# Token norms: the inverse deviation as one power on GpSimd instead of a square root on ScalarE and a reciprocal on VectorE

## The chip, the core and the metric

The kernel runs on one NeuronCore of a Trainium2 chip. The core has five engines that run their own instruction streams and meet only at semaphores: TensorE (PE, matmuls), VectorE (DVE), ScalarE (ACT), GpSimd (POOL) and SyncE (SP, which mostly issues DMAs). The metric is the device time of one execution in microseconds, lower is better.

## The reference

Four layers of gated cross-attention and feed-forward act on a residual stream `x` of 128 x 64 = 8192 tokens of width 128. All eight sub-layers are different computations, but each of them reads a layer norm of the stream, and adds its result to the stream behind a gate:

```python
def _layernorm(x, axis=-1, eps=1e-05):
    m = jnp.mean(x, axis=axis, keepdims=True)
    v = jnp.var(x, axis=axis, keepdims=True)
    return (x - m) / jnp.sqrt(v + eps)

x = x + jnp.tanh(g_xattn[0]) * _L0_xattn_ref(_layernorm(x, axis=-1), ctx_1024, ctx_1024, ...)
x = x + jnp.tanh(g_ffn[0]) * _L0_ffn_ref(_layernorm(x, axis=-1), ...)
...
x = x + jnp.tanh(g_ffn[3]) * _L3_ffn_ref(_layernorm(x, axis=-1), ...)
```

What the change touches is `1 / sqrt(v + eps)`: one number for each token, eight times in the program. With 128 tokens to a tile and one token to a partition, the 8192 numbers are one tile of 128 partitions x 64 columns.

## The kernel before

The stream lives on chip as `X`, 128 partitions x 64 token tiles x 128 features. The program is a sequence of stages, one behind the other: `setup`, and then for each of the eight sub-layers a small stage `norm_header` and the stage or stages of the sub-layer itself. Each stage is a `Stage` object with its own buffers and semaphores, and inside it a block with one stream for each engine. At the end of the block all engines meet; then `Stage.__exit__` has the stage's semaphores cleared on GpSimd (L47) and all engines meet again (L48). No engine starts a piece of the next stage before that, its DMAs included. There is no scheduler: each engine's order is the order in which its function is written.

The sub-layer that last wrote `X` has also put each token's statistics (`bn_stats`: the means and the squared deviations of the even and the odd features) into `S6`. `norm_header` turns these into `m.mean` and `m.rstd`. On VectorE, seven small operations on 128 x 64 tiles (L179 to L187) leave the variance plus epsilon in `spread`. ScalarE waits for the third count of `step`, takes the square root of `spread` into `delta` (L194), and VectorE, which waits for `rooted`, takes the reciprocal of `delta` into `m.rstd` (L189). GpSimd, TensorE and SyncE have nothing to do in this stage. ScalarE's functions come in sets, and a set has to be loaded before its first use: the loads stand in the trace as ACT_TABLE_LOAD, placed by the compiler, with the line of the operation that they serve. The square root is in another set than what comes ahead of it and behind it.

The sub-layers read `m.mean` and `m.rstd` in `normed` (L200), the first piece of work on `X` in each of them.

The last sub-layer has layer norms of its own, in `gated_gelu`. There the inverse deviation of four tiles (128 x 4) is already taken as a power on GpSimd (L2487), with `half_power` a tile filled with -0.5 (L2481):

```python
pool.tensor_tensor(rstd[j][:], var[j][:], half_power[:], ALU.pow).then_inc(rooted[j], 1)
```

Of the kernel before, what the change touches and what calls it, by code (L numbers as in the profile page):

```python
# [12 lines left out]
ALU = mybir.AluOpType  # L13
ACT = mybir.ActivationFunctionType
AX = mybir.AxisListType.X

P = 128
S = 64
NB = 128
NT = NB * S // P  # L20
# [147 lines left out]
def norm_header(nc, m, name, s6=None):  # L168

    s6 = m.S6 if s6 is None else s6  # L170
    with Stage(nc, name) as st:
        delta, spread = st.sb("delta", [P, NT]), st.sb("spread", [P, NT])
        step, rooted = st.sem("step"), st.sem("rooted")

        mean_e, m2_e, mean_o, m2_o = (s6[:, :, k] for k in (1, 2, 4, 5))
        with nc.Block() as block:
            @block.vector
            def _(dve):
                dve.tensor_tensor(m.mean[:], mean_e, mean_o, ALU.add)  # L179
                dve.tensor_tensor(delta[:], mean_e, mean_o, ALU.subtract)  # L180
                dve.tensor_tensor(spread[:], m2_e, m2_o, ALU.add).then_inc(step, 1)
                dve.wait_ge(step, 1)
                dve.tensor_scalar(m.mean[:], m.mean[:], 0.5, None, ALU.mult)
                dve.scalar_tensor_tensor(delta[:], delta[:], 0.25, delta[:], ALU.mult, ALU.mult)
                dve.tensor_scalar(spread[:], spread[:], 1.0 / P, 1e-5, ALU.mult, ALU.add).then_inc(step, 1)
                dve.wait_ge(step, 2)
                dve.tensor_tensor(spread[:], spread[:], delta[:], ALU.add).then_inc(step, 1)  # L187
                dve.wait_ge(rooted, 1)
                dve.reciprocal(m.rstd[:], delta[:])  # L189

            @block.scalar
            def _(act):
                act.wait_ge(step, 3)
                act.activation(delta[:], spread[:], ACT.Sqrt).then_inc(rooted, 1)  # L194


def normed(dve, m, dst, t, src=None):
# [2412 lines left out]
def program(nc, d, stages=None):  # L2610
    with ExitStack() as ctx:
        m = Memory(nc, ctx)
        setup(nc, m, d)
        for n, stage in enumerate(STAGES):
            if stages is None or n in stages:
                norm_header(nc, m, f"norm{n}")
                with ExitStack() as own:
                    stage(nc, m, d, own)
        store(nc, m, d)
# [134 lines left out]
```

## Time and profile before

| what | value |
|---|---|
| median of 3 runs | 3924.22 us (3916.47 to 3931.73) |
| the profiled execution's own time | 3918.53 us |
| span of its instructions | 3916.6 us |
| TensorE busy | 3314.0 us, 85% |
| VectorE busy | 2456.6 us, 63% |
| ScalarE busy | 1686.4 us, 43% |
| GpSimd busy | 1167.3 us, 30% |

The span is what the trace covers, from the first instruction to the last; the execution's own time is 1.9 us longer. Busy shares are averages over very different stages: in a stage where all but one or two engines stand still, they tell nothing of what the stage waits for. The trace is read there in order of time.

### The profile page before, as it was taken

To read this page: it belongs to the slowest core of one execution; us is meant where nothing else is said; L and a number is where in the kernel's file an instruction comes from. 1 tells how busy PE (TensorE), PEld (TensorE's weight loads), DVE (VectorE), ACT (ScalarE), POOL (GpSimd) and SP (SyncE) were. 2 spreads that over 40 slices of the span, in tenths; PEclk is the share of its full clock that TensorE was granted. 3 is DMA by queue.
4 is the path that set the end of the run, shared out by engine and by line. 5 is a ranking of instruction groups with operands and counts; after the bars stand their busy time and mean duration, and the time that the engine had idled before them with its cause. 6 is when DMAs were issued, how large, how long until landed. Compare 5 with 4: busy or idle time off the path is not lost. (4 is left out here: it accounts for less than half of the span.)

```text
span 3916.6 us, 89814 instructions
## 1 busy us (share of the span) xinstructions
PE 3314.0 (85%) x31371; PEld 2123.4 (54%) x31371; DVE 2456.6 (63%) x5197; ACT 1686.4 (43%) x3144; POOL 1167.3 (30%) x1454
## 2 busy tenths in 40 slices
PE   3687999999688795589949997499999779999976
PEld 1464445444566542466646664266666446666644
DVE  7666111111688779878866676777776547777654
ACT  1333222222577536555512223266665226666522
POOL 1664000000233100044410003077775107777510
PEclk8766999999899897799959998799999899999988
DMA  4211000000000005011100002100000110000011
GB/s 131 59 40 51 0 0 0 0 0 0 17 13 13 4 16 226 16 54 45 32 17 1 0 0 74 53 10 9 9 9 4 35 32 10 9 9 9 4 35 56
DMA packets 163476, 107.80 MB, mean 28 GB/s; under 512 B 91390, under 2 KB 151980, under 8 KB 162348
## 3 DMA queue, kind: packets, MB, share of 16 engines
q1 hardware_dynamic: 161788, 104.02, 9.1%
q10 hardware_dynamic: 1584, 2.44, 0.2%
q8 instruction: 59, 0.97, 0.1%
q14 instruction: 45, 0.37, 0.0%
HBM read 68.52 MB, written 16.78 MB: 22 GB/s over the span
## 5 line engine op out<-in xcount | busy, mean ns | idle before, releaser
L2265 POOL TENSOR_TENSOR la_turned<-la_turned,la_sines 128x1024 f32<-128x1024 f32 x128 | 301.7, 2357 | 143.3 <-DVE la_sines L2191 143.3
L908 DVE TENSOR_TENSOR l0f_y<-A,l0f_s 128x512 f32<-128x512 f32 x16 | 11.1, 692 | 463.4 <-PE A L850 463.4
L2259 POOL TENSOR_TENSOR la_scaled<-la_turned,la_rlen 128x1024 f32<-128x1024 f32 x128 | 243.6, 1903 | 16.9 <-POOL la_rlen L2252 13.5
L1175 POOL COPY l1x_vd<-half 128x16 f32<-128x16 f32 x8 | 1.2, 212 | 605.8 <-POOLq L48 605.8
L2161 ACT ACTIVATE la_sq<-A 128x1024 f32<-128x1024 f32 x128 | 131.2, 1025 | 108.1 <-PE A L2311 81.6
L2183 DVE TENSOR_TENSOR la_turned<-A,la_cos 128x1024 f32<-128x1024 f32 x128 | 155.5, 1215 | 29.7 <-issue 15.4
L2145 ACT ACTIVATE la_prob<-la_prob 128x512 f32<-128x512 f32 x128 | 80.7, 630 | 204.1 <-DVE la_prob L2204 204.1
L2499 ACT ACTIVATE gg_gate<-B,gg_b 128x512 f32<-128x512 f32 (+1 forms) x96 | 65.9, 686 | 211.0 <-PE B L2525 211.0
L2201 DVE TENSOR_REDUCE la_top<-B 128x8 f32<-128x512 f32 x128 | 88.6, 692 | 108.4 <-PE B L2324 108.4
L2196 DVE TENSOR_REDUCE la_length<-la_sq 128x16 f32<-128x1024 f32 x128 | 155.1, 1212 | 0.0
L2331 PE MATMUL B<-la_wo,la_oT 128*128 128x128 f32 x1024 | 150.1, 290 | 2.7 <-ACT la_oT L2141 2.7
L2310 PE MATMUL A<-la_wq,la_hT 128*128 128x512 f32 x256 | 136.2, 615 | 11.2 <-DVE la_sines L2191 11.2
L2344 PE MATMUL A<-la_wv,la_hT 128*64 128x256 f32 x1024 | 139.6, 394 | 4.8 <-ACT la_qkT L2122 4.8
L2290 PE MATMUL A<-ident,la_scaled 128*128 128x128 f32 x1024 | 139.5, 279 | 4.4 <-issue 4.4
L2311 PE MATMUL A<-la_wk,la_hT 128*128 128x512 f32 x256 | 134.8, 609 | 0.0
L1506 POOL TENSOR_SCALAR l3x_factor<-l3x_raw 128x256 f32<-128x256 int32 x16 | 14.2, 890 | 398.8 <-DMA l3x_raw<-in_l3x_mask 397.6
L2331 PEld LDWEIGHTS B<-la_wo,la_oT 128*128 128x128 f32 x1024 | 125.5, 193 | 12.0 <-ACT la_oT L2141 3.6
L2524 PE MATMUL A<-gg_hT,gg_w 128*128 128x512 f32 (+1 forms) x192 | 106.1, 635 | 30.4 <-DVE l3f_y L2460 26.6
L2454 DVE SCALAR_TENSOR_TENSOR gg_hid<-A,gg_b,gg_gate 128x512 f32<-128x512 f32 (+1 forms) x96 | 72.0, 750 | 85.2 <-ACT gg_gate L2499 85.2
L2359 PEld LDWEIGHTS B<-la_vd,la_pT 64*64 64x64 f32 x4096 | 71.6, 134 | 97.3 <-issue 97.3
L2290 PEld LDWEIGHTS A<-ident,la_scaled 128*128 128x128 f32 x1024 | 110.0, 141 | 17.2 <-issue 10.4
L1184 POOL TENSOR_TENSOR l1x_kx<-l1x_kT,l1x_head_of 128x512 f32<-128x512 f32 x64 | 66.6, 1040 | 171.2 <-ACT l1x_kT L1303 171.2
(444 smaller groups left out, 9085.8 us busy)
## 6 DMA issues: line engine op xcount, KB each, us to landing
l1f_spill<-l1f_work SPq DMA_DIRECT2D x16, 768.0 KB, 3.2
l1f_xT<-l1f_spill SPq DMA_DIRECT2D x16, 768.0 KB, 6.1
l2x_ctx<-in_ctx SPq DMA_DIRECT2D x128, 64.0 KB, 2.2
memory_vd<-vd SPq DMA_DIRECT2D x64, 68.0 KB
X<-in_x SPq DMA_DIRECT2D x4, 1024.0 KB, 6.5
gates_rows<-in_ctx_rows SPq DMA_DIRECT2D x16, 256.0 KB, 2.8
memory_ctxT<-in_ctxT SPq DMA_DIRECT2D x64, 64.0 KB, 1.9
l1x_ctxT<-in_ctxT SPq DMA_DIRECT2D x64, 64.0 KB
```

The costliest lines, as they stand in the source:

```text
L2161: act.activation(sq[j % 2][:].rearrange("p n c -> p (n c)"), made[:], ACT.Square).then_inc(squared, 1)
L2183: dve.tensor_tensor(heads(turned[j % 2][:]), made_heads, cos[:, :, None, :].broadcast_to([P, 2, HEADS3, W3]), ALU.mult)\
L2196: dve.tensor_reduce(length[j % 2][:], sq[j % 2][:].rearrange("p n (h w) -> p (n h) w", h=HEADS3), AX, ALU.add).then_inc(summed, 1)
L2201: dve.tensor_reduce(top[j % 2][:], sim, AX, ALU.max).then_inc(max_done, 1)
L2259: pool.tensor_tensor(by_head(scaled), by_head(turned), spread_heads(rlen[j % 2][:], W3), ALU.mult)\
L2265: pool.tensor_tensor(turned[j % 2][:], turned[j % 2][:], sines[j % 2][:], ALU.add)\
L2290: last = pe.transpose(keyed[:, n * CH + g * P:n * CH + g * P + P], scaled[j % 2][:, n, g * P:g * P + P], m.ident[:])
L2310: pe.matmul(made[:, 0:CH], hT[j][:], wq[:], start=True, stop=True)
L2311: pe.matmul(made[:, CH:2 * CH], hT[j][:], wk[:], start=True, stop=True).then_inc(qk_made, 1)
L2331: last = pe.matmul(projected, oT[j % 2][:, g], wo[:, g], start=(g == 0), stop=(g == G - 1))
L2344: last = pe.matmul(made_v[u * S:u * S + S, b * G * W3:(b + 1) * G * W3], hT[j][:, b * S:b * S + S], wv[:].rearrange("p (g u w) -> p g u w" ...
L2524: pe.matmul(up_bank(j, o)[0:k], w1[:, n:n + k], hT[j][:], start=True, stop=True)
```

## The change

`norm_header` no longer uses ScalarE. A new tile `half_power` (128 x 64) is filled with -0.5 on GpSimd, which then waits for the third count of `step` and raises `spread` to the power -0.5, straight into `m.rstd`. VectorE's reciprocal and its wait on `rooted` are gone. The other seven operations of VectorE stand as before.

```diff
     with Stage(nc, name) as st:
         delta, spread = st.sb("delta", [P, NT]), st.sb("spread", [P, NT])
-        step, rooted = st.sem("step"), st.sem("rooted")
+        half_power = st.sb("half_power", [P, NT])
+        step, ready = st.sem("step"), st.sem("ready")
...
                 dve.wait_ge(step, 2)
                 dve.tensor_tensor(spread[:], spread[:], delta[:], ALU.add).then_inc(step, 1)
-                dve.wait_ge(rooted, 1)
-                dve.reciprocal(m.rstd[:], delta[:])
-
-            @block.scalar
-            def _(act):
-                act.wait_ge(step, 3)
-                act.activation(delta[:], spread[:], ACT.Sqrt).then_inc(rooted, 1)
+
+            @block.gpsimd
+            def _(pool):
+                pool.memset(half_power[:], -0.5).then_inc(ready, 1)
+                pool.wait_ge(ready, 1)
+                pool.wait_ge(step, 3)
+                pool.tensor_tensor(m.rstd[:], spread[:], half_power[:], ALU.pow)
```

Behind L189 the lines of the changed kernel have numbers that are one higher. Which instructions stand where in each engine's stream is shown at three places. The first is GpSimd around the second token norm, between the last operation of the first sub-layer (L524, L525 in the changed kernel) and the first branch of the next (L778, L779). ISA rows of L47 are the clearing of a stage's semaphores. Before:

```order
L521 TENSOR_TENSOR xnT<-xnT,memory_root 128x512
L524 TENSOR_TENSOR xnT<-xnT,norm_w 128x512
L484 UNCONDITIONAL_BRANCH
L47 ISA x2
L778 UNCONDITIONAL_BRANCH
L47 ISA
```

And in the changed kernel:

```order
L522 TENSOR_TENSOR xnT<-xnT,memory_root 128x512
L525 TENSOR_TENSOR xnT<-xnT,norm_w 128x512
L485 UNCONDITIONAL_BRANCH
L47 ISA
L190 UNCONDITIONAL_BRANCH
L192 MEMSET norm_half_power 128x64
L195 TENSOR_TENSOR rstd<-norm_spread,norm_half_power 128x64
L177 UNCONDITIONAL_BRANCH
L47 ISA
L779 UNCONDITIONAL_BRANCH
```

The fill and the power now stand between two clearings of semaphores, which before followed each other at once. The clearing that ends the norm's stage is behind the power on the same engine.

The second place is VectorE in the same stage. Before:

```order
L184 SCALAR_TENSOR_TENSOR norm_delta<-norm_delta 128x64
L185 TENSOR_SCALAR norm_spread<-norm_spread 128x64
L187 TENSOR_TENSOR norm_spread<-norm_spread,norm_delta 128x64
L189 RECIPROCAL rstd<-norm_delta 128x64
L176 UNCONDITIONAL_BRANCH
L722 UNCONDITIONAL_BRANCH
```

And in the changed kernel:

```order
L185 SCALAR_TENSOR_TENSOR norm_delta<-norm_delta 128x64
L186 TENSOR_SCALAR norm_spread<-norm_spread 128x64
L188 TENSOR_TENSOR norm_spread<-norm_spread,norm_delta 128x64
L177 UNCONDITIONAL_BRANCH
L723 UNCONDITIONAL_BRANCH
```

The reciprocal is gone, and VectorE goes from the addition to the end of the block.

The third place is ScalarE around the sixth token norm, between the attention of the third layer (its exponentials, L1316) and the router of its feed-forward part (L991, an exponential again). Before:

```order
L1289 COPY l2x_oT<-B 128x128 x2
L1150 UNCONDITIONAL_BRANCH
L191 UNCONDITIONAL_BRANCH
L194 ACT_TABLE_LOAD
L194 ACTIVATE norm_delta<-norm_spread 128x64
L176 UNCONDITIONAL_BRANCH
...
L988 UNCONDITIONAL_BRANCH
L991 ACT_TABLE_LOAD
L991 ACTIVATE route_inh<-l2f_mix 128x512
```

And in the changed kernel:

```order
L1290 COPY l2x_oT<-B 128x128 x2
L1151 UNCONDITIONAL_BRANCH
L763 UNCONDITIONAL_BRANCH
...
L989 UNCONDITIONAL_BRANCH
L992 ACTIVATE route_inh<-l2f_mix 128x512
```

Two loads are gone there: that of the square root, and that of the exponential behind it, whose set is still in place. At the seven other norms the square root's load is gone and the next sub-layer's own load stays. TensorE's and SyncE's streams are the same in both kernels.

## Rows read from the trace of the kernel before

**Rows 1.** The page's head: the span, and each engine's busy time.

```profile
span 3916.6 us, 89814 instructions
...
PE 3314.0 (85%) x31371; PEld 2123.4 (54%) x31371; DVE 2456.6 (63%) x5197; ACT 1686.4 (43%) x3144; POOL 1167.3 (30%) x1454
```

**Rows 2.** L187, L189, L194 by themselves: shortest, median, longest ns; first, last start.

```profile
L187 DVE TENSOR_TENSOR norm_spread<-norm_spread,norm_delta x8: 225/226/227, 27.7 to 2501.0; 128x64 f32<-128x64 f32 x8
...
L189 DVE RECIPROCAL rstd<-norm_delta x8: 552/553/554, 28.3 to 2501.5; 128x64 f32<-128x64 f32 x8
...
L194 ACT ACT_TABLE_LOAD  x8: 1283/1283/1283, 26.6 to 2499.8; - x8
L194 ACT ACTIVATE norm_delta<-norm_spread x8: 256/256/257, 28.0 to 2501.2; 128x64 f32<-128x64 f32 x8
```

**Rows 3.** Timeline, second token norm: start, us, engine, line, operation, idle before.

```profile
341.27 0.88 DVE L581 BATCH_NORM_STATS2 S<-X 128x6 f32<-128x128 f32 x4
343.03 1.28 ACT L194 ACT_TABLE_LOAD   x1 [5.99 <-PEq L48]
343.07 0.28 DVE L179 TENSOR_TENSOR mean<-S 128x64 f32<-128x64 f32 x1 [0.93 <-PEq L48]
...
344.20 0.23 DVE L187 TENSOR_TENSOR norm_spread<-norm_spread,norm_delta 128x64 f32<-128x64 f32 x1
344.46 0.26 ACT L194 ACTIVATE norm_delta<-norm_spread 128x64 f32<-128x64 f32 x1 [0.15 <-DVE norm_spread L187]
344.75 0.55 DVE L189 RECIPROCAL rstd<-norm_delta 128x64 f32<-128x64 f32 x1 [0.32 <-ACT norm_delta L194]
346.13 2.14 DVE L200 TENSOR_SCALAR l0f_turn_xn<-X,mean,rstd 128x128 f32<-128x128 f32 x8 [0.82 <-SPq L65]
...
347.30 2.15 PE L745 MATMUL A<-ident,l0f_turn_xn 128*128 128x128 f32 x8 [13.66 <-DVE l0f_turn_xn L200]
```

**Rows 4.** GpSimd's groups by line and shape: busy us, mean ns, idle before.

```profile
L504 POOL TENSOR_TENSOR memory_qx<-xnT,head 128x512 f32<-128x512 f32 x64 | 66.8, 1046 | 48.4 <-PE B L668 48.4
...
L2247 POOL TENSOR_TENSOR la_error<-la_error,la_length 128x16 f32<-128x16 f32 x128 | 28.4, 222 | 10.0
...
L277 POOL MEMSET vd<- 128x512 f32 x1 | 1.0, 1001 | 29.0 <-POOLq L48 29.0
L2481 POOL MEMSET gg_half_power<- 128x4 f32 x2 | 0.2, 101 | 36.8 <-POOLq L48 36.8
```

**Rows 5.** L2487 by itself: the powers that the kernel already takes.

```profile
L2487 POOL TENSOR_TENSOR gg_rstd<-gg_var,gg_half_power x32: 1006/1007/1037, 3046.9 to 3872.8; 128x4 f32<-128x4 f32 x32
```

**Rows 6.** Timeline around the first power.

```profile
3046.62 0.16 DVE L2439 TENSOR_TENSOR gg_var<-gg_var,gg_delta 128x4 f32<-128x4 f32 x1
3046.95 1.04 POOL L2487 TENSOR_TENSOR gg_rstd<-gg_var,gg_half_power 128x4 f32<-128x4 f32 x1 [10.93 <-DVE gg_var L2439]
3048.02 1.12 DVE L2445 TENSOR_SCALAR gg_h<-gg_hs,gg_mean,gg_rstd 128x128 f32<-128x128 f32 x4 [1.24 <-POOL gg_rstd L2487]
```

**Rows 7.** Windows behind five norms: us, busy by engine, granted clock, DMA, GB/s.

```profile
346.00:350.00 4.00, 2.45 (x10) 1.74 (x11) 3.53 (x14) 1.11 (x2) 0.00 (x0) 0.50 0.52 150
...
997.00:1000.00 3.00, 1.97 (x7) 1.48 (x7) 1.45 (x7) 0.00 (x0) 0.45 (x1) 0.50 0.31 86
...
1341.00:1345.00 4.00, 1.97 (x8) 1.58 (x9) 1.35 (x5) 1.88 (x3) 0.00 (x0) 0.50 0.01 2
...
1668.00:1673.00 5.00, 2.91 (x16) 1.67 (x24) 2.03 (x5) 0.53 (x2) 2.72 (x5) 0.50 0.39 104
...
2403.00:2408.00 5.00, 3.33 (x10) 2.29 (x11) 1.19 (x4) 1.17 (x2) 4.66 (x6) 0.50 1.01 208
```

**Rows 8.** Timeline at the start of the router's stage.

```profile
2007.89 1.28 ACT L991 ACT_TABLE_LOAD   x1 [3.60 <-PEq L48]
2007.93 0.16 DVE L952 RECIPROCAL l2f_temp<-l2f_temp 128x1 f32<-128x1 f32 x1 [0.81 <-PEq L48]
2008.13 0.49 DVE L953 TENSOR_SCALAR l2f_mix<-l2f_mix,l2f_temp 128x512 f32<-128x512 f32 x1
2009.19 0.63 ACT L991 ACTIVATE route_inh<-l2f_mix 128x512 f32<-128x512 f32 x1
```

**Rows 9.** Timeline of the first sub-layer: the same four transposes at two times.

```profile
35.50 1.12 PE L416 MATMUL A<-ident,gates_xn 128*128 128x128 f32 x4 [35.50 <-DVE gates_wk L350]
...
53.51 0.66 PE L416 MATMUL A<-ident,gates_xn 128*128 128x128 f32 x4
```

## The prediction

> **What bounds the kernel now.** The page's head says that TensorE is busy for 85% of the span [rows 1], but that average is of no use here. The change lies in eight short stages in which TensorE does nothing, so what counts is the timeline across one of them. Read [rows 3] downward. At 341.27 VectorE takes the last statistics of the first sub-layer; at 343.03 to 343.07 ScalarE and VectorE leave the barrier; VectorE works through its seven small operations until 344.20 + 0.23 = 344.43; ScalarE starts the square root at 344.46, VectorE the reciprocal at 344.75, which ends at 345.30; at 346.13 the next stage's first work on VectorE begins, and at 347.30 TensorE has its first matmul, after 13.66 us of idleness. Nothing else runs between 343.03 and 345.30, and no DMA of the next stage can be issued before the barrier. The norm's stage is therefore one chain of dependent steps, and each microsecond more or less in it moves everything behind it. Eight stages repeat the pattern with the same durations to a few ns [rows 2].
>
> The reader should also see what is not on that chain. ScalarE's table load takes 1283 ns [rows 2], but it starts at the barrier, side by side with VectorE, and ends at 344.31, 0.12 us before VectorE hands over its result [rows 3].
>
> **What is removed.** From the end of L187 to the end of the reciprocal: 345.30 - 344.43 = 0.87 us in each stage (a hand-over of 0.03, the square root 0.26, another 0.03, the reciprocal 0.55) [rows 2, 3]. The load of the square root's set is worth nothing, since VectorE's seven operations cover it; without that cover it would be worth its 1.28 us each time. One more load is gone, that of the router's exponential. There VectorE has the input ready at 2008.13 + 0.49 = 2008.62, the load ends at 2009.17, and the exponential starts at 2009.19 [rows 8]. With the set in place it could start 0.03 us behind VectorE, at 2008.65, so this saves 0.54 us, once.
>
> One rule speaks for a larger gain. The Trainium skill, ScalarE: Activation LUTs, section "What ACT_TABLE_LOAD costs", puts a switch to another set at about 2.66 us, of which some 1.38 us are a drain around the load. The trace agrees with the 1283 ns for the load, and shows no drain on the path: the square root starts 0.03 us after its input is there and 0.15 us after the load [rows 3]. By the page nine switches would be an estimated 24 us off the sum; by the rows they are 0.54 us. I take the rows.
>
> **What is added.** First the fill of `half_power`, 128 x 64, on GpSimd. Bounds from its neighbours are 101 ns for 128 x 4 and 1001 ns for 128 x 512 [rows 4]; on the line between them 64 columns are 0.21 us. It starts at the barrier and VectorE's seven operations last 344.43 - 343.07 = 1.36 us [rows 3], so it is hidden, at either bound; without this cover it would cost its 0.21 us.
>
> Second the hand-over from VectorE to GpSimd. In the existing use of the same pattern VectorE ends at 3046.78 and the power starts at 3046.95: 0.17 us [rows 6]. The barrier takes the place of the hand-over back.
>
> Third the power on 128 x 64, which is the whole question. The trace has it on 128 x 4 alone: 1007 ns, 32 times, from 1006 to 1037 [rows 5]. An ordinary two-input operation of GpSimd takes 222 ns on 128 x 16 and 1046 ns on 128 x 512 [rows 4], that is (1046 - 222) / 496 = 1.66 ns a column and 222 - 16 x 1.66 = 195 ns that do not depend on the size. So a power is no ordinary operation: on a quarter of the columns it takes 4.5 times as long as the 222 ns. How its 1007 ns split into a fixed part and a part for each column can't be read from one size, and 64 columns are 16 times as many as 4. The bounds:
>
> - All of the excess per column: (1007 - 195) / 4 = 203 ns a column, 0.195 + 64 x 0.203 = 13.2 us. If the fixed part is as small as the 101 ns of a tiny fill [rows 4], it is 227 ns a column and 14.6 us.
> - All of the excess fixed, and a column as cheap as in an ordinary operation: 1.007 + 60 x 0.00166 = 1.11 us.
>
> I take 13.2 us. The row that is nearest in kind, the ordinary operation, says that GpSimd's fixed part is some 0.2 us, and a logarithm, a product and an exponential are arithmetic that has to be done for each element. A set-up of 0.8 us, paid once whatever the size, would have no counterpart in any other row of this engine.
>
> **The sum.** Each stage gets longer by 0.17 + 13.2 - 0.87 = 12.5 us, eight of them by 99.8 us (with unrounded terms), less 0.54 us for the router: +99 us. Against the profiled execution's own 3918.5 us that is 4018 us. That execution stood 5.7 us below the median of the runs shown, 3924.2 us, so as a median I expect 4023 us, +2.5%. No cover exists for the 12.5 us: the clearing of the stage's semaphores is queued behind the power on GpSimd, the other four engines wait in the barrier for it, and `normed` (L200), the weights' DMAs and then TensorE are late by as much.
>
> **TensorE's clock** could add to this, since TensorE now idles some 26 us around the second norm in place of 13.66. But behind the norms it restarts at a granted clock of 0.50 (1.2 GHz) as it is: five such windows are in [rows 7], and the sixth and the eighth norm look the same. In the first sub-layer the four transposes take 1.12 us at 35.50 and 0.66 us at 53.51 [rows 9]; so the start is at the lower speed there too. A longer idleness takes nothing from a clock that is already down. When it comes back depends on chance as well, and I allow 10 us either way.
>
> **The rivals.**
> - **Part of the excess is fixed.** Say 0.4 us of the 0.81: then a column costs 103 ns, the power 7.2 us, a stage +6.5 us, the kernel +51 us: 3975 us. For it: some set-up (constants, a call) is likely for such a function. Against it: nothing in the trace shows one. I count powers from 3.2 to 10 us as this case.
> - **The power is nearly flat in size**, so the kernel is not slower. Its place is L195, its price 1.11 us, the lower bound above: 0.17 + 1.11 - 0.87 = +0.41 us a stage, +3.3 - 0.5 = +3 us in all, 3927 us. It decides from a power of 3.2 us downward (37 ns a column), where the eight stages give less than 20 us. For it: other two-input operations do have a slope of only 1.66 ns a column. Against it: it needs a fixed 0.66 us or more that no other GpSimd row has. The Trainium skill, GPSIMD Engine Reference, section 3.1, gives about 2.6 cycles an element for two-input operations, which would put the power here as well; the ordinary operations agree roughly with that, the power on 128 x 4 does not.
> - **The table loads were the real wait**, and the power is nearly flat besides: 9 x 1.28 us come back, 3927 - 11 = 3916 us or less; by the ScalarE page's figure some 24 us, 3903 us. For it: nine loads are gone. Against it: ends and starts in [rows 3] show them covered. For the kernel to be faster by more than 0.5%, both of these would have to hold.
> - **A first power has code to load.** GPSIMD Engine Reference, section 2.1, in the Trainium skill tells of some 6 us for a freshly loaded library. The first of the 32 powers took 1037 ns against a median of 1007 [rows 5], so the trace shows 0.03 us, and I leave it out.
>
> **How the numbers follow.** 0.5% of this time, 20 us, is about what a measurement of this kernel can tell from no change. The steep power (10 to 14.6 us, +74 to +111 us) has 0.60, the partly fixed one 0.22, the flat one 0.15, the loads 0.03. The first two are slower by over 0.5%: 0.82; same 0.15; faster 0.03. The forecast is the first case's, 4023 us. For 8 times in 10 the range has to hold the first two cases: its upper end is 3924 + 111 + 10 = 4045 us. Its lower end is 3950 us, where a power takes about 4 us; below that hardly any of the second case is left. The likeliest case by itself spans 3988 to 4045 us.
>
> **What the next profile would show.** L195: eight powers, each near 13.2 us (the sum is right), near 7 (partly fixed) or near 1.1 (flat). The eight durations should be equal to some tens of ns. The power should start 0.17 us behind VectorE's last addition, with all other engines idle under it. GpSimd's busy time grows by 8 x 13.4 = 107 us. ACT_TABLE_LOAD rows: nine fewer, without a gain beyond the router's 0.54 us. The idle time of TensorE ahead of its first matmul at the second norm grows from 13.66 to about 26 us. The prediction would be wrong if the power has a small slope, if something of the next stage starts under it, or if TensorE's clock comes back much earlier or later behind several norms.

## The result, and the profile after

The changed kernel takes 3992.99 us (median of 4, 3991.79 to 3999.28), the kernel before beside it 3920.34 us (median of 4). The ratio is 1.0185, with a 95% interval of 1.0158 to 1.0212: +73 us, slower. The forecast was 4023 us, +99 us. One execution of all those reported below, 4073.87 us in the kernel with the logarithm (mean granted clock 0.87, where the others of that kernel have 0.92), is in none of the ratios.

The page of the profiled execution after, head and busy times (as in [rows 1]):

```profile
span 3992.0 us, 89815 instructions
...
PE 3309.3 (83%) x31371; PEld 2120.1 (53%) x31371; DVE 2453.5 (61%) x5189; ACT 1672.0 (42%) x3127; POOL 1251.4 (31%) x1470
```

The span is 75.4 us longer, and the only engine with more work is GpSimd, by 84.1 us. The groups of its powers and of the fill by line and shape (busy us, mean ns, idle before), and below them the new power by itself (L2488 is the power that the kernel before has at L2487):

```profile
L195 POOL TENSOR_TENSOR rstd<-norm_spread,norm_half_power 128x64 f32<-128x64 f32 x8 | 84.5, 10564 | 11.2 <-DVE norm_spread L188 11.2
L2488 POOL TENSOR_TENSOR gg_rstd<-gg_var,gg_half_power 128x4 f32<-128x4 f32 x32 | 32.2, 1007 | 270.8 <-DVE gg_var L2440 270.8
L192 POOL MEMSET norm_half_power<- 128x64 f32 x8 | 1.2, 151 | 1442.4 <-POOLq L48 1056.7 <-ACTq L177 385.7
```

```profile
L195 POOL TENSOR_TENSOR rstd<-norm_spread,norm_half_power x8: 10549/10560/10583, 27.8 to 2567.2; 128x64 f32<-128x64 f32 x8
```

The power on 128 x 64 takes 10.56 us; the eight norms, with different data, lie within 0.04 us of each other. The timeline of the second norm, to be read beside [rows 3]:

```profile
352.62 0.15 POOL L192 MEMSET norm_half_power<- 128x64 f32 x1 [2.57 <-POOLq L48]
352.67 0.27 DVE L180 TENSOR_TENSOR mean<-S 128x64 f32<-128x64 f32 x1 [0.98 <-PEq L48]
...
353.80 0.23 DVE L188 TENSOR_TENSOR norm_spread<-norm_spread,norm_delta 128x64 f32<-128x64 f32 x1
354.18 10.58 POOL L195 TENSOR_TENSOR rstd<-norm_spread,norm_half_power 128x64 f32<-128x64 f32 x1 [1.40 <-DVE norm_spread L188]
365.61 2.14 DVE L201 TENSOR_SCALAR l0f_turn_xn<-X,mean,rstd 128x128 f32<-128x128 f32 x8 [11.59 <-SPq L65]
...
366.78 1.50 PE L746 MATMUL A<-ident,l0f_turn_xn 128*128 128x128 f32 x5 [23.60 <-DVE l0f_turn_xn L201]
```

From the first operation of the norm to the first `normed` it is now 365.61 - 352.67 = 12.94 us, where it was 346.13 - 343.07 = 3.06 us: +9.88 us in one stage. TensorE's wait ahead of its first matmul went from 13.66 to 23.60 us. Under the power all other engines stand still, so eight such stages are 79 us.

The traces bear that out for the whole program. Take in each norm the time from its first operation on VectorE (L179, L180 in the changed kernel) to the first operation on `X` that reads the inverse deviation. The eight such stretches, called the norms' stages from here on, add up to 49.9 us in the trace before and to 129.0 us in the trace after: +79.1 us. All the rest of the program takes 3866.8 us before and 3863.0 us after. The loss lies in the norms' stages and nowhere else.

The router, as in [rows 8]:

```profile
2062.96 0.48 DVE L954 TENSOR_SCALAR l2f_mix<-l2f_mix,l2f_temp 128x512 f32<-128x512 f32 x1
2063.48 0.63 ACT L992 ACTIVATE route_inh<-l2f_mix 128x512 f32<-128x512 f32 x1 [4.35 <-DVE l2f_mix L954]
```

No load stands ahead of the exponential any more, and it starts 0.04 us behind its input, where it had started 0.57 us behind it: 0.53 us back, once.

### The profile page after: what moved, and what is told of

It is laid out like the page before. It is cut to its first block and busy times, and to the rows that moved or that the text cites. A ratio compares the mean times of both kernels' runs of the same rounds, so it can differ in the third digit from the quotient of the medians.

```text
span 3992.0 us, 89815 instructions
## 1 busy us (share of the span) xinstructions
PE 3309.3 (83%) x31371; PEld 2120.1 (53%) x31371; DVE 2453.5 (61%) x5189; ACT 1672.0 (42%) x3127; POOL 1251.4 (31%) x1470
## 5 line engine op out<-in xcount | busy, mean ns | idle before, releaser
L2488 POOL TENSOR_TENSOR gg_rstd<-gg_var,gg_half_power 128x4 f32<-128x4 f32 x32 | 32.2, 1007 | 270.8 <-DVE gg_var L2440 270.8
```

## The experiments

The theory (A): the whole loss is the power's own duration on a path that nothing covers, a fixed part and a part for each column. Its rivals were another law of the size (B), a price of the move to GpSimd as such (C), table loads that had been on the path after all (D), and a price of TensorE's longer idleness in its clock (E).

### The law of the size

```diff
-                pool.tensor_tensor(m.rstd[:], spread[:], half_power[:], ALU.pow)
+                w = {"norm0": 1, "norm1": 2, "norm2": 4, "norm3": 8, "norm4": 16, "norm5": 32, "norm6": 48}.get(name, 64)
+                for n in range(0, NT, w):
+                    cols = slice(n, min(n + w, NT))
+                    pool.tensor_tensor(m.rstd[:, cols], spread[:, cols], half_power[:, cols], ALU.pow)
```

> The eight token norms of the changed kernel take the same 64 columns of powers in pieces, one behind the other: 64 pieces of 1 column in the first norm, 32 of 2 in the second, 16 of 4, 8 of 8, 4 of 16, 2 of 32, 48 + 16 in the seventh, and 64 in one in the eighth. The result is the same. Theory A (a fixed 0.37 us and 159 ns a column, the straight line through 1.007 us at 4 columns and 10.56 us at 64): 0.53 us for 1 column, 0.69 for 2, 1.01 for 4, 1.64 for 8, 2.92 for 16, 5.46 for 32, 8.0 for 48. Rival B (a column costs 203 ns when there are few and less when there are many, with 0.2 us fixed, a curve): 0.40 for 1, 0.60 for 2, and above the line in between, 1.8 for 8, 3.4 for 16.

GpSimd's groups of this kernel, by shape:

```profile
L198 POOL TENSOR_TENSOR rstd<-norm_spread,norm_half_power 128x1 f32<-128x1 f32 x64 | 32.4, 540 | 1.4 <-DVE norm_spread L188 1.4
L198 POOL TENSOR_TENSOR rstd<-norm_spread,norm_half_power 128x2 f32<-128x2 f32 x32 | 21.1, 697 | 1.4 <-DVE norm_spread L188 1.4
...
L198 POOL TENSOR_TENSOR rstd<-norm_spread,norm_half_power 128x4 f32<-128x4 f32 x16 | 15.7, 1008 | 1.4 <-DVE norm_spread L188 1.4
L198 POOL TENSOR_TENSOR rstd<-norm_spread,norm_half_power 128x16 f32<-128x16 f32 x5 | 14.4, 2899 | 1.4 <-DVE norm_spread L188 1.4
L198 POOL TENSOR_TENSOR rstd<-norm_spread,norm_half_power 128x8 f32<-128x8 f32 x8 | 12.8, 1637 | 1.4 <-DVE norm_spread L188 1.4
L198 POOL TENSOR_TENSOR rstd<-norm_spread,norm_half_power 128x32 f32<-128x32 f32 x2 | 10.8, 5431 | 1.4 <-DVE norm_spread L188 1.4
L198 POOL TENSOR_TENSOR rstd<-norm_spread,norm_half_power 128x64 f32<-128x64 f32 x1 | 10.6, 10574 | 1.4 <-DVE norm_spread L188 1.4
L198 POOL TENSOR_TENSOR rstd<-norm_spread,norm_half_power 128x48 f32<-128x48 f32 x1 | 8.0, 8019 | 1.4 <-DVE norm_spread L188 1.4
```

The eight sizes lie on one straight line, each within 0.04 us of theory A's number. From 4 to 64 columns the slope is (10574 - 1008) / 60 = 159 ns a column, and 1008 - 4 x 159 = 0.37 us don't depend on the size; the step from 1 to 2 columns is 157 ns as well. B is out. The kernel as a whole took 4042 us in its one run: the 0.37 us are paid 129 times in place of 8, which by this line is 45 us.

### The move without the power

```diff
-                pool.tensor_tensor(m.rstd[:], spread[:], half_power[:], ALU.pow)
+                pool.tensor_tensor(m.rstd[:], spread[:], half_power[:], ALU.mult)
```

> The changed kernel with the power replaced by a multiplication by half_power, so the inverse deviation is not computed (the norms are scaled wrongly). All else is as in the changed kernel: hand-over to GpSimd, the fill, nine table loads fewer, no reciprocal. Theory A (all of the loss is the power's own duration): a 128x64 multiplication takes 0.3 us, each stage gets 0.17 + 0.30 - 0.87 = -0.40 us, the kernel -3.7 us against before, the same within noise. Rival C (moving work to GpSimd and its barrier costs something of its own): slower than before. Rival D (the table loads had been on the path): 11 us or more faster than before.

3909.65 us (median of 10) against 3919.26 us (13), ratio 0.9974 [0.9964, 0.9985], that is -10.2 us [-14.1, -5.9]. The multiplication by itself:

```profile
L195 POOL TENSOR_TENSOR rstd<-norm_spread,norm_half_power x8: 317/318/319, 27.7 to 2490.6; 128x64 f32<-128x64 f32 x8
```

With 0.32 us on GpSimd the kernel is faster than before, so the move as such costs nothing and C is out. The gain is larger than the 3.7 us that A gives it, which is why the table loads were tried by themselves below. In the norms' stages the price is A's: they add up to 46.8 us in this trace, 3.1 us less than in the first trace of before (A: 8 x 0.40 = 3.2). The rest of the gain lies outside the norms.

### Half the columns, and the power twice

```diff
-                pool.tensor_tensor(m.rstd[:], spread[:], half_power[:], ALU.pow)
+                pool.tensor_tensor(m.rstd[:, 0:32], spread[:, 0:32], half_power[:, 0:32], ALU.pow)
```

(and on VectorE, behind the last addition, `dve.tensor_copy(m.rstd[:, 32:64], spread[:, 32:64])`)

> The changed kernel with the power on 32 of the 64 columns; the other half of the inverse deviations is a copy of the variance made by VectorE beside it, so half of the tokens are scaled wrongly. Theory A (duration on the path, a line in the size): the power takes 5.46 us, the kernel is 8 x 5.1 = 41 us faster than the changed one, that is 3920 + 73 - 41 = 3952 us, ratio to before 1.008. Rival E (a good part of the 73 us is something else, such as a slower clock of TensorE behind a longer idle stretch): the gain is clearly less than 41 us.

```diff
                 pool.tensor_tensor(m.rstd[:], spread[:], half_power[:], ALU.pow)
+                pool.tensor_tensor(spare[:], spread[:], half_power[:], ALU.pow)
```

> The changed kernel with a second power of the same size on GpSimd behind the first one in each norm, into a tile that nothing reads. Theory A: +8 x 10.5 = +84 us over the changed kernel, 4077 us, ratio to before 1.040. Rival E (the idle stretch costs more or less than its length, by the clock): clearly off 84 us in the direction of its cost.

| kernel | on GpSimd in each norm | median | ratio to the runs of before beside it |
|---|---|---|---|
| multiplication | 0.32 us | 3909.65 us | 0.9974 [0.9964, 0.9985] |
| power on 32 columns | 5.44 us | 3958.21 us | 1.0095 [1.0070, 1.0120] |
| changed kernel (five more runs) | 10.56 us | 3991.03 us | 1.0185 [1.0163, 1.0207] |
| power twice | 21.1 us | 4082.22 us | 1.0423 [1.0399, 1.0447] |

From the first row to the last GpSimd has 20.8 us more in each of eight norms, 166 us, and the kernel is 172.6 us longer: 1.04 us for each microsecond of the operation, and the intervals of the two ratios leave the 172.6 some 10 us either way. Half was 6 us above its expectation, twice 5 us above. Whether such differences belong to the power is seen in the traces, where the norms' stages can be taken apart from the rest:

| trace | eight norms' stages | all the rest |
|---|---|---|
| multiplication | 46.8 us | 3857.1 us |
| before, first and second trace | 49.9 and 50.5 us | 3866.8 and 3865.6 us |
| power on 32 columns | 87.9 us | 3873.3 us |
| changed kernel, first and second trace | 129.0 and 128.9 us | 3863.0 and 3859.9 us |
| power twice | 213.4 us | 3856.8 us |

From the multiplication to the power twice the stages grow by 166.6 us, the operation's own 166 us, and the rest is the same to 0.3 us. The rest scatters by 16.5 us, and not in the order of the power. The largest piece of that is the stretch from the end of the third norm's stage to the fourth norm. It takes 340.1 us with the power on 32 columns, and 333.8 and 328.6 us in the two traces of before, which are one and the same program; TensorE's granted clock is at 1.2 GHz for 50.0, 33.5 and 21.4 us of it. So the power costs its duration, and the scatter around it comes with TensorE's clock elsewhere.

### The changed kernel again, and with the square root kept beside the power

> The changed kernel once more, unchanged, so that it stands on the same chip and beside the same runs of before as the three kernels of this group. Theory A, with the power at its measured 10.56 us: 8 x (0.17 + 10.56 - 0.87) - 0.54 = +78 us. Rival D (some 6 us of the nine table loads had been on the path, as the multiplication's gain of 9.6 us where 3.7 were expected would have it): +72 to +73 us, as the changed kernel showed before.

3991.03 us (median of 5), ratio 1.0185 [1.0163, 1.0207], that is +72.5 us [+64, +81]. The middle of the ratio is the number that D named (the two medians themselves are 69.9 us apart), but A's +78 us is inside the interval too, so this run doesn't tell them apart.

```diff
+            @block.scalar
+            def _(act):
+                act.wait_ge(step, 3)
+                act.activation(spare[:], spread[:], ACT.Sqrt)
```

> The changed kernel, and beside the power ScalarE takes the square root of the same tile into a tile that nothing reads, so that all nine table loads are back while the power covers the one in the norm's stage. The result is the same. Theory A (loads are hidden but for the router's): +0.5 us over the changed kernel, the same. Rival D (the loads had cost some 6 us): if they cost through the next sub-layers' own loads, +6 us; if through the norm's stage itself, the same here too.

3996.28 us (median of 5), ratio 1.0196 [1.0178, 1.0213], +5 us over the changed kernel, with intervals that overlap for the most part. All 44 loads of the kernel before are back in its trace (35 in the changed kernel's), and the norms' stages add up to 129.1 us, as in the changed kernel: in the norms the loads are covered. The time of the whole is inconclusive by itself; the next one is the cleaner test.

### The loads taken away, the chain left

```diff
-                act.activation(delta[:], spread[:], ACT.Sqrt).then_inc(rooted, 1)
+                act.activation(delta[:], spread[:], ACT.Identity).then_inc(rooted, 1)
```

> The kernel before, with ScalarE copying the variance (an identity, which needs no table of its own) in place of the square root, so the inverse deviation is wrong. All of the chain stays, hand-overs and reciprocal included; nine table loads are gone. Theory A: -0.5 us against before, the same. Rival D (loads on the path): -6 us or more, ratio 0.998 or less.

3918.96 us (median of 11) against 3921.15 us (21), ratio 0.9996 [0.9986, 1.0007]: -1.6 us [-5.5, +2.7]. Nine loads fewer are worth no more than noise. D is out as it was stated, at 6 us or more; anything from nothing to 5 us remains possible.

### What an exposed load costs

```diff
-                dve.wait_ge(rooted, 1)
-                dve.reciprocal(m.rstd[:], delta[:])
...
-                act.activation(delta[:], spread[:], ACT.Sqrt).then_inc(rooted, 1)
+                act.activation(delta[:], spread[:], ACT.Ln).then_inc(rooted, 1)
+                act.wait_ge(rooted, 1)
+                act.activation(m.rstd[:], delta[:], ACT.Exp, scale=-0.5)
```

> The kernel before, with the inverse deviation on ScalarE alone: a logarithm, and behind it an exponential of -0.5 times it, without VectorE's reciprocal. The compiler places two loads in each norm, the logarithm's (covered by VectorE's seven operations) and the exponential's between the two, with no cover; four of the next sub-layers' own loads of the exponential's set go. It shows what an exposed load costs. By the 1283 ns of a load alone, the end of the stage moves by 0.03 + 1.28 + 0.26 - 0.58 = +1.0 us in each of eight, +8 us less the router's 0.5: ratio 1.002. If a drain of 1.4 us comes on top of an exposed load, +2.4 us a stage, +18 us, ratio 1.005.

3925.85 us (median of 10; 3925.25 us without the one execution named at the result), ratio 1.0009 [0.9997, 1.0022]. The timeline of its first norm:

```profile
27.48 0.22 DVE L187 TENSOR_TENSOR norm_spread<-norm_spread,norm_delta 128x64 f32<-128x64 f32 x1
27.74 0.26 ACT L192 ACTIVATE norm_delta<-norm_spread 128x64 f32<-128x64 f32 x1
28.01 1.28 ACT L194 ACT_TABLE_LOAD   x1
29.31 0.26 ACT L194 ACTIVATE rstd<-norm_delta 128x64 f32<-128x64 f32 x1
```

The load starts as the logarithm ends (28.00) and the exponential starts 0.02 us behind the load's end. An exposed load costs its 1.28 us and no drain on top. In the second norm the compiler placed neither load, and the exponential follows the logarithm at once:

```profile
349.49 0.26 ACT L192 ACTIVATE norm_delta<-norm_spread 128x64 f32<-128x64 f32 x1 [7.42 <-DVE norm_spread L187]
349.77 0.26 ACT L194 ACTIVATE rstd<-norm_delta 128x64 f32<-128x64 f32 x1
```

That norm's stage is 0.3 us shorter than before (2.75 against 3.06 us), and the stages of the seven norms that paid the load are 0.8 to 1.3 us longer. The eight together grow by 7.1 us (57.0 against 49.9), inside the +3.5 us [-1, +9] of the whole.

### The kernel before against itself

> The kernel before, unchanged, as one of the compared kernels. It shows how far two equal kernels fall apart here, and gives a second trace of the kernel before. Ratio 1.000 within 0.2%. If the 4 to 5 us that every changed kernel's trace has less than expected between the fourth and the fifth norm belong to a chance dip of TensorE's clock in the one trace of before, this trace has 325 us there in place of 329.7; if they belong to the change, it has 329 to 330 us again.

3918.70 us (median of 11), ratio 0.9998 [0.9989, 1.0007]. From the start of the fourth norm to that of the fifth the trace of before has 329.7 us and this one 329.7 again, while the kernels of this study with a changed norm had some 2 to 5 us less there than their added durations ask for, but for the changed kernel with a busy TensorE below. By the words of the expectation that speaks for an effect of the change and against chance; what the other traces say of it follows. The place is a gap of 1.57 us in TensorE's work in the feed-forward part. The same four matmuls and the window around them, first the kernel before:

```profile
1437.47 0.27 PE L1970 MATMUL B<-ident,l1f_highest 128*2 128x128 f32 x1 [1.57 <-DVE l1f_highest L1794]
...
1438.88 3.78 PE L1977 MATMUL A<-l1f_xT,l1f_wT 128*128 x4
```

```profile
1437.00:1447.00 10.00, 8.90 (x15) 4.06 (x16) 2.06 (x12) 2.23 (x2) 0.00 (x0) 0.66 0.00 0
```

and the kernel with an identity in place of the square root:

```profile
1437.59 0.27 PE L1970 MATMUL B<-ident,l1f_highest 128*2 128x128 f32 x1 [1.57 <-DVE l1f_highest L1794]
...
1438.79 1.98 PE L1977 MATMUL A<-l1f_xT,l1f_wT 128*128 x4
```

```profile
1437.00:1447.00 10.00, 8.79 (x22) 4.09 (x23) 2.92 (x13) 3.97 (x4) 0.00 (x0) 1.00 0.00 0
```

In the first the granted clock falls to 1.2 GHz behind the gap (mean 0.66) and four matmuls take 3.78 us in place of 1.98; from the small matmul to the first sigmoid (L1921) it is 1451.46 - 1437.47 = 13.99 us against 1448.38 - 1437.59 = 10.79 us. So 3.2 us hang on whether the clock falls here. The gap is 1.57 us in all thirteen traces. The clock fell behind it in both traces of before and in the changed kernel with a busy TensorE (13.99, 13.99 and 14.02 us, mean clock 0.66), partly in the changed kernel's first trace (12.40 us, 0.83), and not in the other nine (10.80 us, 1.00), among them the changed kernel's second trace and the kernel with an identity, whose norms' stages (50.2 us) are as long as those of before. So the gap alone doesn't decide it. The changed kernel has it both ways, and the kernel before only one way in two traces; whether that is chance or the exact moment at which the stretch begins stays open. In the traces it takes 2.3 and 4.7 us off the changed kernel's stretch from the fourth norm's stage to the fifth norm (321.1 and 318.8 us, 323.4 before), and 5.3 us off the multiplication's (318.1 us). With the 3.1 us of the norms' stages that leaves 3 to 4 us of the multiplication's gain in its trace open; its norms also hand other values on, and no run tells what that does.

### TensorE kept busy under the norm

```diff
+            @block.tensor
+            def _(pe):
+                for _ in range(10):
+                    pe.matmul(m.A_all[:, 0:CH], m.ident[:], m.X[:, 0:TPC, :].rearrange("p t k -> p (t k)"),
+                              start=True, stop=True)
```

> The changed kernel with ten 128x512 matmuls on TensorE in each norm, beside the power, into a bank of PSUM that is overwritten afterwards. The result is the same. Theory A (behind the norms the clock is down in both kernels, the 10 us of idleness cost only their length): if the matmuls bring the clock up or keep it up, the sub-layers' starts get shorter, but that would be a gain over both kernels, at most half of TensorE's work in the low stretches behind the norms, some 5 to 15 us in all. Rival E (the idle stretch costs clock beyond its length): also faster than the changed kernel, and the low-clock stretches come down to those of before or below. If the clock doesn't react, the same as the changed kernel.

3992.63 us (median of 5), ratio 1.0185 [1.0171, 1.0200]: the same as the changed kernel. Three windows of it, under the power of the second norm, at the next stage's first matmul, and behind that:

```profile
353.00:363.00 10.00, 10.00 (x20) 4.14 (x18) 0.22 (x1) 0.00 (x0) 9.63 (x1) 0.78 0.00 0
365.00:367.00 2.00, 0.66 (x5) 0.42 (x5) 2.00 (x9) 0.33 (x1) 0.00 (x0) 1.00 0.30 44
368.00:378.00 10.00, 8.46 (x32) 5.72 (x32) 8.42 (x31) 4.38 (x8) 0.00 (x0) 0.50 0.85 307
```

The transposes at the start of that stage:

```profile
365.97 0.66 PE L752 MATMUL A<-ident,l0f_turn_xn 128*128 128x128 f32 x4 [2.54 <-DVE l0f_turn_xn L207]
367.00 0.66 PE L752 MATMUL A<-ident,l0f_turn_xn 128*128 128x128 f32 x4 [0.37 <-DVE l0f_turn_xn L207]
368.11 2.13 PE L752 MATMUL A<-ident,l0f_turn_xn 128*128 128x128 f32 x8 [0.45 <-DVE l0f_turn_xn L207]
```

The clock did come up under the power and the first eight transposes ran at 2.4 GHz (0.66 us for four), but then it fell to 0.50 again (2.13 us for eight), and the kernel won nothing. Together with the power twice, where the rest of the program is no longer than with the multiplication, this says that the idle stretch costs its length and no more; E is out.

The kernel before, with the same block and `range(2)`:

> The kernel before with two such matmuls on TensorE in each norm, about 2 us at the lower speed, beside the 2.3 us of the norm's chain. The result is the same. Theory A: too little to change the clock, the same as before. If it does bring the clock up earlier, faster than before by some microseconds.

3928.30 us (median of 11), ratio 1.0015 [1.0004, 1.0026], +6 us. The expectation had the size of the matmuls wrong:

```profile
343.64 3.75 PE L199 MATMUL A<-X,ident 128*128 128x512 f32 x4 [9.43 <-PEq L48]
...
345.33 0.55 DVE L189 RECIPROCAL rstd<-norm_delta 128x64 f32<-128x64 f32 x1 [0.32 <-ACT norm_delta L194]
348.20 1.11 DVE L206 TENSOR_SCALAR l0f_turn_xn<-X,mean,rstd 128x128 f32<-128x128 f32 x4 [2.32 <-SPq L65]
```

Each of the two calls is two matmuls in the trace, together they took 3.75 us at the lower speed, and ended 1.5 us behind the reciprocal. TensorE became the last one at the barrier, and the next stage began 348.20 - 343.64 = 4.56 us behind the norm's start in place of 3.06. Seven of the eight stages are longer by 1.1 to 1.8 us. The third is not (12.91 against 12.73 us): there the granted clock is up, the same four matmuls take 1.96 us, and they end ahead of the reciprocal:

```profile
988.52 1.96 PE L199 MATMUL A<-X,ident 128*128 128x512 f32 x4 [2.61 <-PEq L48]
990.21 0.55 DVE L189 RECIPROCAL rstd<-norm_delta 128x64 f32<-128x64 f32 x1 [0.32 <-ACT norm_delta L194]
```

The eight stages together grow by 10.5 us (60.4 against 49.9). The trace as a whole grows by 5.7 us, since the clock did not fall in the gap described above (318.5 against 323.4 us in that stretch). That makes the point of the study once more: the engine that ends last in this stage is paid in full, and one that ends earlier costs nothing.

## Why the prediction was right, and where it was off

**The chain.** Right. The norm's stage is one chain between two barriers. What was removed (0.87 us) stands in the trace as taken, the hand-over was 0.15 us where 0.17 had been taken, and the stage grew by 9.88 us: 0.15 + 10.58 - 0.87 = 9.86.

**The fill.** Right: 0.15 us (0.21 had been estimated), under VectorE's seven operations, and the power waited for VectorE (L188) all eight times.

**The table loads.** Right. They were covered: without them the kernel is the same (0.9996), and with them back beside the power the norms' stages are too (129.1 against 129.0 us). The rule of the Trainium skill, ScalarE: Activation LUTs, section "What ACT_TABLE_LOAD costs", that a switch costs some 2.66 us with its drain, held neither for a covered load nor for an exposed one, which cost 1.28 us. Measured here, the load's duration stands and the drain does not.

**The power.** This is the term that was mis-sized: 13.2 us expected, 10.56 us measured. The step was "All of the excess per column". The excess of 0.81 us over an ordinary operation on 4 columns was 0.17 us fixed and 0.64 us for the columns (159 ns each), not 0.81 for the columns (203 ns each). From one size the split could not be read; the fixed part, 0.37 us where an ordinary operation has 0.20, was what the first rival named, only smaller. The direction, the place and the law (a straight line) were right. An extrapolation by 16 turned 0.17 us of error in the fixed part into 2.6 us of the result, and eight norms into 21 us. Some luck is in it as well. From one size the power could be anything from 1.11 to 14.6 us. The argument that picked the upper end spoke of a logarithm, a product and an exponential for each element; no run shows by what arithmetic GpSimd takes a power, only that a column costs 159 ns.

**The sum.** With the measured power it gives 8 x (0.17 + 10.56 - 0.87) - 0.54 = +78 us; measured were +73 us and +72.5 us, with intervals of 62 to 83 and 64 to 81. In the two traces of each kernel the norms' stages did grow by 78.4 to 79.1 us, as the sum has it, and all else was 3 to 7 us shorter, 2.3 to 4.7 us of that where the clock fell before and fell less or not at all after. That these few microseconds made the measured time smaller than the sum is nothing that the prediction had foreseen.

**The clock.** Right that the longer idleness costs nothing beyond its length. The allowance of 10 us either way was enough.

**The rivals.** The flat power, and with it "not slower", did not come: a column of the power costs 159 ns, not 1.66 ns. The multiplication on 128 x 64, with 0.32 us, does keep to the slope of the ordinary operations. Code to load ahead of a first power was rightly left out: the first of the eight starts 0.14 us behind its input and is as short as the others.

```profile
27.38 0.23 DVE L188 TENSOR_TENSOR norm_spread<-norm_spread,norm_delta 128x64 f32<-128x64 f32 x1
27.75 10.55 POOL L195 TENSOR_TENSOR rstd<-norm_spread,norm_half_power 128x64 f32<-128x64 f32 x1 [1.40 <-DVE norm_spread L188]
```

## What to carry to other kernels

An operation that moves to an idle engine is free only under cover; in a stage where everybody waits for it at a barrier, its whole duration is paid: that the engine had nothing else to do hides nothing. A price known at one small size has to be split into its fixed and its per-column part before it is scaled up, and one trace with the sizes 1 to 64 in it does that in a single run. Taking out table loads gains nothing where the load starts with the stage and its input comes later: look at which of the two ends last.

## What the runs showed of the hardware that was not expected

- GpSimd's element-wise power costs 0.37 us plus 159 ns a column of 128 partitions, from 1 to 64 columns; a multiplication of 128 x 64 takes 0.32 us in the same place.
- A table load between two activations costs 1.28 us, with 0.02 us around it.
- Behind one gap of 1.57 us in a stretch that is otherwise full of matmuls, the same in thirteen traces, the granted clock fell to half in three of them, for a shorter time in one and not in nine; where it fell fully, 3.2 us were lost. Two traces of the changed kernel differ in it.
- The stretch from the third norm's stage to the fourth norm, in the same program, took 333.8 us in one trace and 328.6 us in another, with TensorE at 1.2 GHz for 33.5 and for 21.4 us of it. Over all kernels of the study this stretch, in which their instructions are the same, took 328 to 340 us, by and large the longer the more of it was at 1.2 GHz (21 to 50 us).
- With matmuls under the power of the second norm the granted clock was 1.00 at the next stage's first transposes (365 to 367 us) and 0.50 again in its thinner work (368 to 378 us), and no time was won.
